# A two-layer graph network on one core: a ring of 16 gathered groups for the first half of the second layer, residual rows read again, and a GpSimd program without loops

## What is computed

```python
msg = h[edge_src] + relvectors[edge_rel]                    # layer one, h = x
red = segment_sum(msg, edge_dst)
x   = layernorm(x + gru_cell(red, x, w_ih, w_hh, b_ih, b_hh))
deg = segment_sum(ones, src);  s = rsqrt(deg)               # layer two, with loops added
out = segment_sum(s[src] * s[dst] * (x @ W.T)[dst], src)
x   = layernorm(x + out)
```

## Time and profile before

| | us |
|---|---|
| median of three runs | 2945.31 (2928.23 to 2953.8) |
| span of the profiled execution | 2217.2 |
| median less the span | 728.1 |
| busy: PE, DVE, POOL | 1944.7, 1710.1, 1611.8 |

### The profile page before, as it was taken

The page is one execution under the profiler, slowest core; times in us unless marked ns, Lnnn a source line. Parts: engine busy times, 40 slices in busy tenths (PEclk is TensorE's granted clock), DMA queues, the critical chain, the costliest instruction groups (busy, mean ns, idle before and its releaser), DMA issues.

```text
span 2217.2 us, 42539 instructions
## 1 busy us (share of the span) xinstructions
PE 1944.7 (88%) x9408; PEld 1477.5 (67%) x9408; DVE 1710.1 (77%) x2998; ACT 910.1 (41%) x3071; POOL 1611.8 (73%) x1763
## 2 busy tenths in 40 slices
PE   4699888799999999999977998888988988777997
PEld 3577666567777766777755886666766766565886
DVE  5499989999999968888867997677857877444676
ACT  1100000246666644444436884376815876000123
POOL 6777777777777776776655777777777777777773
PEclk8899999899999999999988999999999999999999
DMA  5355555444444455666655333333333333333335
GB/s 147 110 168 171 171 166 167 128 141 143 143 143 142 137 159 170 190 184 206 198 155 162 106 106 106 104 106 106 105 104 106 107 106 105 104 106 106 106 105 162
DMA packets 134043, 302.47 MB, mean 136 GB/s; under 512 B 31152, under 2 KB 67530, under 8 KB 133664
## 3 DMA queue, kind: packets, MB, share of 16 engines
q0 software_dynamic: 79872, 218.21, 34.3%
q10 hardware_dynamic: 43508, 71.27, 9.6%
q1 hardware_dynamic: 10444, 10.38, 1.5%
HBM read 267.74 MB, written 38.40 MB: 138 GB/s over the span
## 4 chain that ended last, share of the span: by engine, by line
PE 31%; POOL 30%; issue 18%; DVE 11%; DVEq 4%; DMA 4%; ACT 2%; SPq 0%; POOLq 0%; ACTq 0%
POOL rows L580 29%; PE ps L1718 18%; PE ps L1914 4%; DMA rows<-gdram,ids 2%; DVE sums L885 2%; PE ps L1916 2%; PE ps L1934 1%; DVE sums L948 1%; PE ps L1904 1%; PE ps L1864 1%; DVEq L805 1%; DVE onehot L783 1%; DVEq L790 1%; PE ps L1782 1%; DVEq L802 1%
## 5 line engine op out<-in xcount | busy, mean ns | idle before, releaser
L1718 PE MATMUL ps<-rows,onehot 128*128 x5632 | 1350.0, 393 | 157.2 <-SPq L436 86.2
L1718 PEld LDWEIGHTS ps<-rows,onehot 128*128 128x128 f32 x5632 | 1062.1, 193 | 382.5 <-issue 209.5
L580 POOL DMA_INDIRECT rows<-in_x_dram,ids x832 | 796.8, 958 | 271.7 <-issue 240.5
L580 POOL DMA_INDIRECT rows<-gdram,ids x832 | 788.5, 948 | 282.8 <-issue 228.5
L868 DVE TENSOR_TENSOR sums<-sums,ps 128x256 f32 x400 | 167.2, 418 | 302.2 <-PE ps L1718 284.5
L839 DVE SCALAR_TENSOR_TENSOR onehot<-tkey,node_p,ps 128x512 f32<-128x512 f32 x403 | 298.1, 740 | 9.2 <-issue 5.2
L885 DVE TENSOR_TENSOR sums<-ps,sums 128x800 f16<-128x800 f32 (+1 forms) x156 | 215.4, 1414 | 1.2 <-issue 1.2
L783 DVE SCALAR_TENSOR_TENSOR onehot<-tkey,node_p,ps 128x1024 f32<-128x1024 f32 x152 | 193.2, 1271 | 2.2 <-DVE steps_i L762 1.0
L1458 ACT ACTIVATE wT<-wT,a 128x208 f16<-128x208 f16 x312 | 116.1, 454 | 172.9 <-DVE wT L777 172.9
L1403 ACT COPY sums<-ps 128x256 f32<-128x256 f32 x49 | 18.2, 372 | 345.1 <-PE ps L1774 345.1
L1458 ACT ACTIVATE onehot<-bias,a 128x208 f16<-128x208 f16 x312 | 116.1, 454 | 69.5 <-DVE bias L777 64.0
(11 more groups left out here) (287 smaller groups left out, 2029.8 us busy)
## 6 DMA issues: line engine op xcount, KB each, us to landing
xpd<-sums ACTq DMA_DIRECT2D x48, 384.0 KB, 3.4
sums<-xpd ACTq DMA_DIRECT2D x48, 384.0 KB
rows<-in_x_dram,ids POOLq DMA_INDIRECT x832, 2.9
rows<-gdram,ids POOLq DMA_INDIRECT x832, 2.8
xt<-in_x_dram ACTq DMA_DIRECT2D x96, 128.0 KB, 2.4
gdram<-in_x_dram ACTq DMA_DIRECT2D x5, 1250.0 KB
gdram<-sums ACTq DMA_DIRECT2D x48, 128.0 KB
out_dram<-sums SPq DMA_DIRECT2D x5, 896.0 KB
```

The costliest lines, as they stand in the source:

```text
L580: pool.indirect_dma_start(rows[:, at:at + D], None, source, bass.IndirectOffsetOnAxis(ap=lists(n, p)[:, s * h + k:s * h + k + 1], axis=0)) ...
L1718: prod = M.matmul(ps[:, h, 0:width], onehot[:, u % U, k, :], rows[:, bass.ds(at + k * stride, width)], start=(k == 0), stop=(k == q - 1))
```

## The change

It has three parts.

1. **The ring.** `rows` and `sums0` become parts of one tile `arena`. In layer two's first 104 groups (SPLIT1, the first two chunks) the ring has 16 groups (WIDE1): of each 16, the first eight are gathered into `sums0`, whose sums layer one has used up by then, and the other eight into `rows`. The 32 semaphores stay as they are, so GpSimd also waits, before a group, for the arrival of the group eight before it. SP gives out the first eight places once `bring` has copied 31 tiles (SPARE), and the other eight as layer one's last groups are released. Towards group 104 SP gives out nothing for eight releases, and from there the ring has eight groups. TensorE works out which half a group lies in with one more register step and one more address step in each of the first 200 steps.
2. **The residual.** `put_g` no longer writes into `sums0`. After group 104 SP reads the rows of `gdram` back into `sums0` (`own_again`, seven DMAs of up to seven tiles, and two for the last tile). These rows are x times s, so `whole` multiplies them by 1/s squared (the tile `deg`) instead of multiplying the product by s; what it leaves is the sum divided by s, and `collect` and `final_roots` set this right (`deg_inv`, `deg_rs`), with two more small DVE instructions for each call of `final_roots`.
3. **GpSimd's program** is written out: no loops, no `ids`, the indices read from `tidx` itself, and the padding column not gathered in either layer.

```diff
+COLS = -(-E // P)
...
+WIDE1 = 2 * RING1
+SPLIT1 = 2 * (C // CH // H1)
+SPARE = -(-RING1 * H1 * D // W0)
...
+        deg, deg_inv = sb("deg", [P, NT]), sb("deg_inv", [P, NT])
+
+        ahead_of = (S * H + 1) * RS - R
+        arena = sb("arena", [P, ahead_of + B * W0])
+        rows, sums0 = arena[:, 0:ahead_of], arena[:, ahead_of:ahead_of + B * W0]
...
-            for s in range(RING1 // 2):
+            sp.wait_ge(s_redc, SPARE)
+            sp.sem_inc(s_free[1], RING1)
+            for s in range(S):
                 released(0, free_i, NG - S + s, J)
-                sp.sem_inc(s_free[1], 2)
-
-            first_groups(1, RING1, H1)
-            groups(1, free1_i, CH * NG1, RING1, H1, CH * J1)
+                sp.sem_inc(s_free[1], RING1 // S)
+
+            def own_again(t):
+
+                tiles = min(FG, NT - 1 - t)
+                sp.dma_start(sums0[:, t * W0:(t + tiles) * W0].rearrange("p (s w) -> p s w", w=W0)[:, :, 0:D],
+                             gdram[t * P:(t + tiles) * P, :].rearrange("(s p) d -> p s d", p=P)).then_inc(s_again, 16)
+
+            for group in range(RING1):
+                arrived(1, group)
+            sp.wait_ge(s_plan_rd, 2)
+            for group in range(CH * NG1 - RING1):
+                released(1, free1_i, group, CH * J1)
+                if group < SPLIT1 - WIDE1 + RING1 or group >= SPLIT1:
+                    sp.sem_inc(s_free[1], 1)
+                elif group == SPLIT1 - 1:
+                    for k in range(2):
+                        sp.wait_ge(s_gst[k], (NT + 1 - k) // 2 * 16)
+                        sp.sem_inc(s_go, 1)
+                if SPLIT1 <= group < SPLIT1 + NT // FG:
+                    own_again((group - SPLIT1) * FG)
+                if group == SPLIT1 + NT // FG:
+                    for p, z in LAST_PARTS:
+                        sp.dma_start(sums0[p:z, (NT - 1) * W0:(NT - 1) * W0 + D],
+                                     gdram[(NT - 1) * P + p:(NT - 1) * P + z, :]).then_inc(s_again, 16)
+                if group < SPLIT1:
+                    arrived(1, group + RING1)
+                elif group >= SPLIT1 + RING1 // 2:
+                    arrived(1, group + RING1 // 2)
+            for group in range(CH * NG1 - RING1 // 2, CH * NG1):
+                arrived(1, group)
 
...
-            stage(0, S * H, s_tidx, 0, 0)
-            with pool.Fori(0, NG // S // 2) as i:
-                for p in range(2):
-                    issue(0, x[:, :], S, H, RS, s_tidx, i * 2 + p, p)
-
-            pool.wait_ge(s_ids[0], C // (S * H) + 1)
...
+            for grp in range(NG):
+                pool.wait_ge(s_free[0], grp + 1)
+                pool.sem_inc(s_go, 1)
+                for k in range(min(H, COLS - grp * H)):
+                    slot, column = grp % S * H + k, grp * H + k
+                    pool.indirect_dma_start(
+                        rows[:, slot * RS:slot * RS + D], None, x[:, :],
+                        bass.IndirectOffsetOnAxis(ap=tidx[:, column:column + 1], axis=0)).then_inc(s_rows[slot], 16)
 
             for g in range(CH):
-                a = g * turns
-                stage(1, S1 * H1, s_tix, a, a % 4)
+                pool.wait_ge(s_tix, g + 1)
                 if g == 1:
                     for k in range(2):
                         pool.wait_ge(s_gst[k], (NT + 1 - k) // 2 * 16)
-                with pool.Fori(0, turns // 4) as i:
-                    for p in range(4):
-                        issue(1, gdram[:, :], S1, H1, D, s_tix, i * 4 + (a + p), (a + p) % 4, base=half(a + p))
-                issue(1, gdram[:, :], S1, H1, D, s_tix, a + turns - 1, (a + turns - 1) % 4, False, half(a + turns - 1))
+                for grp in range(g * NG1, (g + 1) * NG1):
+                    pool.wait_ge(s_free[1], grp + 1)
+                    if grp < RING1:
+                        pool.wait_ge(s_grp[0], NG - S + 1 + grp * H1 // H)
+                    else:
+                        pool.wait_ge(s_grp[1], grp - RING1 + 1)
+                    pool.sem_inc(s_go, 1)
+                    for k in range(min(H1, COLS - grp * H1)):
+                        slot, column = grp % RING1 * H1 + k, grp * H1 + k
+                        place = (sums0 if grp < SPLIT1 and grp % WIDE1 < RING1 else rows)[:, slot * D:slot * D + D]
+                        pool.indirect_dma_start(
+                            place, None, gdram[:, :],
+                            bass.IndirectOffsetOnAxis(ap=tidx[:, column:column + 1], axis=0)
+                        ).then_inc(s_rows[slot], 16)
...
-                V.scalar_tensor_tensor(part, ps[:, (5, 7)[t % 2], 0:D], deg_rs[:, t:t + 1], sums0[:, t * W0:t * W0 + D],
+                V.scalar_tensor_tensor(part, sums0[:, t * W0:t * W0 + D], deg[:, t:t + 1], ps[:, (5, 7)[t % 2], 0:D],
                                        ALU.mult, ALU.add).then_inc(s_whole, 1)
...
-                note(V.tensor_scalar(ve_all[:, bass.ds(t, tiles)], mv_all[:, 0:tiles, 1], EPS, None, ALU.add))
+                note(V.tensor_tensor(ve_all[:, bass.ds(t, tiles)], mv_all[:, 0:tiles, 1], deg_inv[:, bass.ds(t, tiles)],
+                                     ALU.mult))
                 note(V.tensor_scalar(mean_all[:, bass.ds(t, tiles)], mv_all[:, 0:tiles, 0], -1.0, None, ALU.mult))
...
+                step(V.tensor_scalar(ve_all[:, part], ve_all[:, part], EPS, None, ALU.add))
                 step(V.tensor_scalar(half_all[:, part], ve_all[:, part], -0.5, None, ALU.mult))
                 roots(rs_all[:, part], ve_all[:, part], half_all[:, part], sq_all[:, part], root_all[:, part], ALU.add)
+                step(V.tensor_tensor(rs_all[:, part], rs_all[:, part], deg_rs[:, part], ALU.mult))
                 step(V.tensor_tensor(mean_all[:, part], mean_all[:, part], rs_all[:, part], ALU.mult))
...
+                    dve.wait_ge(s_again, (NT // FG + 2) * 16)
...
                 A.activation(g_out[:, k, :], yc[:, m, :], ACT.Identity,
                              scale=rd[:, bass.ds(t, 1)]).then_inc(s_gev, 1)
-                A.activation(sums0[:, bass.ds(t * W0, D)], yc[:, m, :], ACT.Identity,
-                             scale=rs[:, bass.ds(t, 1)]).then_inc(s_x1, 1)
                 act.wait_ge(s_gev, t + 2)
...
                 at = ((group - 1) & (ring - 1)) * (q * stride)
+                if n and wide:
+                    at = at + ((group + (RING1 - 1)) & RING1) * (ahead_of // RING1)
+                    at = at.with_bounds(min_val=0, max_val=ahead_of + (RING1 - 1) * H1 * D)
...
-                        walk_step(1, D, i * body + (first + u), u)
+                        walk_step(1, D, i * body + (first + u), u, i * body + (first + u) < CH // 2 * J1)
```

93 lines of the change are left out of this document (31 added, 62 removed).

## The result

The changed kernel took 3028.47 us (median of 4, 3009.96 to 3039.77) against 2947.80 of the kernel before (2928.23 to 2953.80): a ratio of **1.029** [1.025, 1.034].

What follows compares the result with a forecast made beforehand. After a start set by PE and DVE, GpSimd's gathers were taken to bound the kernel until 2057 us, then a PE tail. The stream's -38.1 us and DVE's +1.7 gave -36.4, so 2945.3 became 2909 us, range 2888 to 2944.

Steps and rivals of the forecast that it cites:

- The 728 us: Outside the profiled span: the median's 728.1 us above the 2217.2 us span, taken as fixed and unchanged.
- the first rival: Whole timed execution stretched by 1.33 against the profile, so the gain is 48 us, giving 2897 us; chance 15%.
- GpSimd's stream of gathers: Layer two: sets the time until 2057 us at 1.2515 us a gather, 1040.0 us for 831 intervals.
- That is 2.7 us of room: Chunk two's seam: `extract` writes indices at 1363.8 us, the new stream wants them at 1366.5.
- Narrowing the ring again at group 104 costs nothing: End of chunk two: group 104 released at about 1637 us, wanted at 1666.9, so 30 us of room.
- All four stalls go: Start of layer two: the wider ring removes four GpSimd waits for SP's release, together 28.1 us.
- The start: Layer two's first gather: forecast at 1106.2 us, against 1108.59 in the kernel before.
- reload with residual: SP's nine added DMAs cost nothing at the end; two more DVE steps per `final_roots` call cost 1.7 us.
- Written-out gathers: Rival on GpSimd's program: written-out gathers cost more to issue, 0.08 us each giving +30 us, 2975 us; chance 8%.
- Time outside growing with the program: Rival outside the span: six per cent more instructions add 45 us, giving 2954 us; chance 7%.
- Ring not wider in effect: Rival in layer two: SP or the `s_grp` wait holds GpSimd at eight groups, 28.1 us return, 2937 us; 6%.
- Address steps: Rival on PE: 0.17 us for 80 steps delays `extract` by 13.6 us, gain 25 us, 2920 us; chance 13%.

Runs made afterwards that it cites:

- the straight kernel: Kernel before with only GpSimd's program written out, without loops or index copies: 0.995 to 0.998 where the kernel before took about 2219 us, 1.000 (2937.07 us) against 2944.26.
- a room of eight: Changed kernel with layer two's ring room taken back to eight groups throughout, all else kept: 2927.74 us, 1.0045 of the kernel before (2911.83).
- the seams' run: Changed kernel with SP's program reordered at the layers' seam and at the ring's narrowing: 2182.34 us, 0.983 of the kernel before (2219.11).
- wide to group 32: Changed kernel with room for 16 groups only until group 32 of layer two, eight from there: 2193.06 and 2191.05 us, 0.9885 and 0.9877 of the kernel before.

## Why the prediction was wrong

**The step that failed** is "The median is 728.1 us above the span, and no row shows why; I take that part as fixed". There is no such part: time less span is 1.7 to 2.0 us in either manner. The 728 us are spread over the program, as the first rival had it in its premise. But that rival then stretched the gain by 1.33, and the sign was what changed.

The sum was made of the waits of an execution that the timed ones don't resemble, and what it put at nothing there (TensorE beside a denser stream of gathers, at the start of layer two, behind `extract` and behind the second seam) took 19.4 + 36.3 + 16.1 us.

The Trainium skill's section on the launch (Runtime: NRT & Kernel Launch, "The ~15µs preamble/postamble breakdown") puts the launch at 9 to 15 us. The forecast concluded from it that a launch can't account for 728 us, and the runs agree; the page's figure itself isn't in the difference of time and span, which is 2.0 us at most.

**What bounds layer two** is another thing in a timed execution. The forecast had "GpSimd's stream of gathers" at 1.2515 us each, 1040 us. The free manner bears it out: 1042.6 us for the changed kernel's 830 intervals. Stopping, the straight kernel needs 1325 us for 831, 1.59 each. TensorE and SP run slower there (80 steps of the walk take 258 us against 190 free); GpSimd waits for SP in 103 places for 298.5 us in all.

**"That is 2.7 us of room" at `extract`.** Free about right, as the seams' run shows. Stopping, the wide ring lets GpSimd come 35.6 us early, since TensorE, which carries `extract`, is slower and GpSimd isn't. With a room of eight it came 10.6 us late there (the gather is at 1904.8 us, the indices are written at 1894.2).

**"Narrowing the ring again at group 104 costs nothing", with "the room is 30 us".** Free it cost 3.1 us and not by TensorE: SP waits for the arrival of group 111 ahead of the release of 104, a thing queued behind SP's wait that the sum didn't look for. Stopping it cost 33.3 us, because TensorE came out of the gapless gathers more than eight groups behind. Behind it the walk's last 200 steps lost 0.4 and 4.6 us in the two traces.

**"All four stalls go"**: yes, free. Stopping, the straight kernel has stops of 32.0 and 4.5 us in its first 11 groups, and the changed one, with twice the room, has them of 16.3 and 24.0 us in its first 17. Counted from the first gather, the changed kernel's 65th is 10 us sooner than the straight kernel's and its 208th 2 us: the room saved next to nothing even there, and TensorE began layer two 21 us later.

**The terms of the sum, free.** Forecast -36.4 us, measured -29.3. The start came 2.5 us later than 1106.2 and the narrowing took 3.1; these are 5.6 of the 7.1. Of the 2.5 a part is chance: in the two free traces of the kernel that is wide to group 32, the same up to there, the first gather is at 1106.1 and 1107.4. The straight program gave 5 to 11 us where the copies in layer two had been put at 6, and reload with residual cost 2 to 5 where 1.7 stood. The mechanism was right there, the size was off.

**The rivals.** Written-out gathers: refuted in both manners (0.995, 1.000), and 0.95 us a gather as before. Time outside growing with the program: refuted; the executed instructions even fell, from 42,539 to 42,320, and the two counts of the built programs that it starts from stand in no trace. Ring not wider in effect: refuted by the missing stops. Address steps: nothing to be seen free (`extract` at 1362.5 to 1366.8 us in the four free traces with them, at 1361.2 to 1364.7 in the twelve without; in three of them the walk's first 80 steps take 189.5 to 189.9 us, before 189.6), and inside the 0.45% of the kernel with a room of eight when stopping. The forecast's 12% for slower was given for written-out gathers and time outside the span. No rival had the mechanism that decided.

**Shown and argued.** Shown: the room of the ring makes the loss in the stopping manner; TensorE loses the time in three places (the start of layer two, and behind either chunk seam), each beside a run of gathers without a gap, in both traces of the changed kernel; and it loses nothing in between. Argued, from those two traces: that the gathers are the cause of TensorE's standing still. No run issued the same gathers with gaps put in between. Open: through what they would hold it up, and what makes an execution stop or run free. In the stopping traces 20 to 27% of the chain is put down to "another core or an unknown queue", in the free ones none of it; work of other cores of the chip is recorded nowhere and so not ruled out. The core's two instruction queues moved 100 and 131 packets in a stopping execution of the changed kernel and in a free one alike, so they don't tell, and comparisons on the same chip number fell on either side. No profile of the unchanged kernel itself in a stopping execution was taken.

**The better version** depends on the manner: free, the one with the seams moved beats both (0.983 against 0.987). Stopping, none that was run (changed, straight, room of eight) beats the kernel before.

## What to carry to other kernels

Set the profiled time beside the timed ones before anything else: a gap of hundreds of microseconds between them is no constant to carry along, but says that the trace shows another execution than the one you are asked about. A wider ring lets a producer run ahead, and it is worth its room only until the next wait that the producer can't pass (here the node indices of the next chunk); behind such a wait it comes back as a burst. Whether a burst costs anything was here a matter of the manner: nothing free, most of the loss stopping. A long wait of the producer is no cost in itself; follow the consumer's own steps to see where the end is lost. Where one sequencer serves several waits in a fixed order, look at what stands between a release and the wait for it.

## What the hardware showed unexpectedly

- The same program takes 2219 us or 2912 to 2948, whole comparisons long. In the slower manner register instructions of TensorE's sequencer take 0.70 us beside gapless gathers, where they take 0.046 in the faster.
- There, one gather every 1.25 us without a gap left TensorE 16 matmuls in 25 us; with 4 to 10 gathers in 25 us it made 87 to 114; both traces of the changed kernel have it. In the free manner TensorE is busy 91% at the full rate of gathers.
- The gathers themselves are alike in both: 946 ns median, 0.30 us behind each.
